# Rotating q and k in place in the attention loop of a decoder block, and moving one ScalarE copy

## The reference

```
x1 = layernorm(x  + mamba(x))                     # projection, causal conv, selective scan, gate, projection
x2 = layernorm(x1 + retention(x1, ctx))           # cross attention, no softmax
x3 = layernorm(x2 + experts(x2))                  # shared expert + top 2 of 8 routed experts
```

```
q = xpos(x1  @ Wq)                      # 256 features
k = xpos(ctx @ Wk, inverse_scale=True)
v = ctx @ Wv
scores = (q @ k.T) * decay_mask         # 128 x 128 in each sequence
out    = scores @ v

xpos(x) = x * cos_table + rotate_half(x) * sin_table
```

## Time and profile before

| | |
|---|---|
| time, median of 3 runs | 1811.83 us |
| profiled execution, its own time | 1807.94 us |
| its span in the profile | 1805.9 us |
| mean granted TensorE clock (share of 2.4 GHz) | 0.978 |
| PE busy | 1685.7 us (93%) |
| DVE busy | 1208.9 us (67%) |
| ACT busy | 805.4 us (45%) |
| POOL busy | 730.1 us (40%) |
| front stage | about 0 to 553 us |
| attention loop | about 553 to 1123 us |
| routed experts | about 1123 us to the end |

### The profile page before, as it was taken

One profiled execution on the slowest core, in us unless ns is written; L12 is line 12 of the kernel. 1 busy time (PEld: TensorE's weight loads), 2 busy tenths in 40 slices (PEclk: granted clock), 3 DMA queues, 4 the chain that ended last, 5 costly groups with the idle time before them and its releaser, 6 DMA issues.

```text
span 1805.9 us, 36443 instructions
## 1 busy us (share of the span) xinstructions
PE 1685.7 (93%) x9652; PEld 1434.9 (79%) x9653; DVE 1208.9 (67%) x2735; ACT 805.4 (45%) x1507; POOL 730.1 (40%) x673
## 2 busy tenths in 40 slices
PE   6999977999986999999999996999999999999995
PEld 4777746888875888888888874888888888888884
DVE  6888866788874676676677667555555555556554
ACT  5788856777732323323323324333333333333332
POOL 1111105888852345434435435233333333333333
PEclk9999988999998999999999998999999999999998
DMA  4555574778853232232233226334544444444444
GB/s 143 182 181 192 193 256 131 231 240 248 269 189 121 84 117 97 92 115 101 84 111 113 83 86 242 55 55 84 107 93 90 103 92 92 97 100 89 93 108 103
DMA packets 155373, 237.54 MB, mean 132 GB/s; under 512 B 41824, under 2 KB 119840, under 8 KB 146992
## 3 DMA queue, kind: packets, MB, share of 16 engines
q1 hardware_dynamic: 129728, 201.29, 34.4%
q0 software_dynamic: 25584, 35.54, 11.2%
HBM read 131.11 MB, written 105.64 MB: 131 GB/s over the span
## 4 chain that ended last, share of the span: by engine, by line
PE 56%; POOL 4%; issue 3%; DVE 3%; DMA 1%; ACT 1%; SPq 0%; POOLq 0%; ACTq 0%; DVEq 0%
PE block_banks L2873 21%; PE block_banks L2893 11%; PE block_banks L2772 5%; PE block_banks L2758 4%; PE block_banks L2882 3%; PE block_banks L2749 3%; POOL attention_turned_qk L2055 2%; PE block_banks L2675 2%; PE block_banks L2704 2%; PE block_banks L2861 2%; PE block_banks L2712 2%; POOL sorted L2044 1%; PE block_banks L2663 1%; PE block_banks L2693 1%; DVE back_w_down L2264 1%
## 5 line engine op out<-in xcount | busy, mean ns | idle before, releaser
L2873 PE MATMUL block_banks<-back_w_gu,back_xe_T 128*128 x1620 | 412.6, 403 | 4.8 <-DVE back_xe_T L2572 4.7
L2873 PEld LDWEIGHTS block_banks<-back_w_gu,back_xe_T 128*128 128x128 f32 x1620 | 297.4, 189 | 64.9 <-issue 5.6
L2893 PE MATMUL block_banks<-back_w_down,back_he_T 128*128 x1620 | 225.4, 288 | 1.5 <-DVE back_he_T L2584 1.5
L2893 PEld LDWEIGHTS block_banks<-back_w_down,back_he_T 128*128 128x128 f32 x1620 | 200.8, 188 | 1.8 <-issue 1.7
L1445 PE MATMUL block_banks<-front_xn_T,front_w_in_parts 128*128 128x512 f32 x768 | 187.9, 401 | 5.2 <-issue 3.3
L2087 POOL DMA_INDIRECT more<-back_y,back_token x67 | 103.9, 1551 | 216.5 <-DVE back_y L2591 198.6
L2044 POOL DMA_INDIRECT sorted<-back_x,back_slot x128 | 128.6, 1005 | 139.3 <-DVE back_slot L2389 91.2
L2087 POOL DMA_INDIRECT acc<-back_y,back_token x68 | 107.6, 1583 | 179.2 <-DVE back_y L2591 162.4
L1445 PEld LDWEIGHTS block_banks<-front_xn_T,front_w_in_parts 128*128 128x128 f32 x768 | 144.2, 191 | 42.5 <-issue 6.3
L1262 DVE SCALAR_TENSOR_TENSOR front_conv<-block_banks,front_conv_wb,front_conv 128x508 f32<-128x508 f32 (+2 forms) x192 | 140.8, 740 | 44.5 <-ACT front_conv L1075 38.6
L2223 ACT ACTIVATE back_he_T<-block_banks 128x512 fp32r<-128x512 f32 x135 | 80.8, 599 | 199.7 <-PE block_banks L2882 199.7
(11 more groups left out here) (267 smaller groups left out, 3113.3 us busy)
## 6 DMA issues: line engine op xcount, KB each, us to landing
back_xe<-sorted SPq DMA_DIRECT2D x135, 136.0 KB
gate_T<-front_gate_T SPq DMA_DIRECT2D x16, 1024.0 KB, 4.8
xc_T<-front_xc_T SPq DMA_DIRECT2D x16, 1024.0 KB, 5.8
front_xc_in<-xc_T SPq DMA_DIRECT2D x16, 1024.0 KB, 5.3
front_gate_in<-gate_T SPq DMA_DIRECT2D x16, 1024.0 KB, 6.6
front_x_rows<-in_x SPq DMA_DIRECT2D x16, 512.0 KB, 5.6
front_c_rep<-c_parts SPq DMA_DIRECT2D x128, 64.0 KB, 4.5
front_rows_in<-in_x SPq DMA_DIRECT2D x16, 512.0 KB, 7.7
```

What stands on the lines that cost most here:

```text
L2873: op = nc.tensor.matmul(dst[:, r % 2], xe_T[:, x_part, k], w_gu[:, bass.ds(e, 1), m, w_part, k], start=(n == 0), stop=(n == len(PASSES) - 1))
L2893: op = nc.tensor.matmul(ps_y[:, 0:D_MODEL], he_T[:, h_part, k], w_down[:, bass.ds(e, 1), w_part, k], start=(n == 0), stop=(n == len(DOWN_P ...
```

## The change

Two edits, both in the attention loop of `decoder_back`.

1. q and k each get two `parts` buffers of their own. DVE writes the two cosine products straight into `turned_qk`, where the sums are to stand, and the two sine products into `parts[2*which]` and `parts[2*which+1]`. POOL then adds or subtracts in place: `turned_qk` is an input and the output. DVE's wait for POOL's sums is now the same for q and k: those of the group before (`4 * a`). The wait for `scores_done` moves from POOL to DVE, which is now the first to write `turned_qk`.
2. On ACT, `chunk_high` moves from before the logits' copy to behind it.

```
@@ GpSimd, step @@
                     for which in range(0 if is_at(a, 0) else 2):
                         pool.wait_ge(parts_ready, 8 * a + 4 * which + 4)
-                        pool.wait_ge(scores_done, a)
                         for half, op in enumerate((ALU.subtract, ALU.add)):
-                            nc.gpsimd.tensor_tensor(turned_qk[:, which, half], parts[:, 2 * half], parts[:, 2 * half + 1],
-                                                    op).then_inc(xpos_ready, 1)
+                            nc.gpsimd.tensor_tensor(turned_qk[:, which, half], turned_qk[:, which, half],
+                                                    parts[:, 2 * which + half], op).then_inc(xpos_ready, 1)
@@ ScalarE, step @@
-                if expert and attention and u:
-                    chunk_high((g - 1) // 2)
-                if is_at(expert and g, GROUPS - 2):
-                    chunk_high(EARLY)
                 if is_at(expert and g, GROUPS - 1):
                     act.wait_ge(scores_done, GROUPS)
                     for c in range(8, 11):
...
                     nc.scalar.activation(logits_T, ps_small[0:2 * EXPERTS], ACT.Copy).then_inc(logits_T_ready, 1)
+                if expert and attention and u:
+                    chunk_high((g - 1) // 2)
+                if is_at(expert and g, GROUPS - 2):
+                    chunk_high(EARLY)
@@ VectorE @@
             def xpos_parts(a, which):
                 done, cos, sin = ((q_done, "q_cos", "q_sin"), (k_done, "k_cos", "k_sin"))[which]
-                dve.wait_ge(xpos_ready, 4 * a + 2 * which)
-                for i, half, table in ((0, 0, cos), (3, 0, sin), (1, 1, sin), (2, 1, cos)):
+                dve.wait_ge(xpos_ready, 4 * a)
+                dve.wait_ge(scores_done, a)
+                for dst, half, table in ((turned_qk[:, which, 0], 0, cos), (parts[:, 2 * which + 1], 0, sin),
+                                         (parts[:, 2 * which], 1, sin), (turned_qk[:, which, 1], 1, cos)):
                     dve.wait_ge(done, 2 * a + half + 1)
-                    nc.vector.tensor_tensor(by_seq(parts[:, i]), by_seq(ps_wide[:, half]), per_seq(tables[table]),
+                    nc.vector.tensor_tensor(by_seq(dst), by_seq(ps_wide[:, half]), per_seq(tables[table]),
                                             ALU.mult).then_inc(parts_ready, 1)
```

## The result

The changed kernel takes 1800.61 us (median of 7 runs, 1798.62 to 1806.36) against 1811.38 us for the kernel before in the same comparison (7 runs, 1809.32 to 1814.26). The ratio is 0.995, with a 95% interval from 0.9936 to 0.9963: 9.1 us less (6.7 to 11.6). On the 1811.83 us that the forecast started from, this is 1802.8 us. The forecast was 1804.0 us. The direction and the mechanism held; the size was too small, and what sits behind that size is the interesting part.

The account below looks back on a forecast made before the run. PE, busy 436.27 of 443 us in the attention loop, was taken to set the pace. Its waits, 3.1 + 2.6 + 2.1 = 7.8 us, off the median 1811.83 us gave 1804.0 us; range 1801 to 1809 us.

Parts of the forecast that it names:

- The waits at the logits, the score and the up projection: PE's only idle places in the attention loop from 604 to 1080 us: 3.1, 2.6 and 2.1 us, all to go.
- DVE's new wait for the scores: Before DVE writes the products, twice a step: claimed always met, since that score product starts over 20 us earlier.
- x1's low part: DVE's input to q's projection, ending 0.36 us before it: closest on PE, claimed to move forward with the removed waits.
- The slowed products of k: DVE's k products beside POOL's sums: at most 1.1 us each instead of 0.62, then ending at 787.33, as late as now.
- The term of the rotation: k's products no longer wait for POOL's sums of q; PE's score and up projection waits go: 2.6 + 2.1 = 4.7 us.
- The two starts agree with the idle time in brackets: Up projection to score: 1.90 us in an even step, 1.51 in an odd one, taken as without a wait; difference 0.39.
- Together 7.8 us. That is what there is to win: Sum of PE's listed idle time at three places in the attention loop, taken as all that could be won.
- the copy: ACT's logits' copy exchanged with a chunk's rounding in odd steps: PE's wait before the logits' transposes goes, 3.1 us.
- rival 1: One edit doesn't pay: k products slowed beside POOL, 1808.7 us; or the copy still waits, 1807.1 us. Chance 0.07 together.
- The second rival: Another PE wait in the loop takes their place, first x1's low part; if all is lost again, 1811.8 us. Chance 0.07.
- wrong on the sum if a new waiter stands in PE's list: The prediction's own sign against its 7.8 us: a new entry among PE's waits in the loop.
- What was to show it: Signs in the new profile: PE's three waits gone or each under 0.5 us, a middle step about 0.4 us less.

Follow-up runs that it names:

- the rotation alone: Edit to q/k buffers, in-place sums and DVE's waits, without moving ACT's chunk behind the logits' copy, against the kernel before: 1806.34 us, ratio 0.9968.
- the second profiles of the two kernels: Both kernels run again unchanged: the changed one 1803.05 us, ratio 0.9947 to the kernel before; a single run of the one before 1808.59 us.

## Why the prediction was right, and where its size was off

- **The places and the mechanism: right.** The waits at the logits, the score and the up projection went. The price in place is nil (1302 against 1304 ns), DVE's products and POOL's sums don't slow each other, DVE's new wait for the scores holds nothing, and x1's low part, the closest input by 0.36 us, never became a wait of PE. (The slowed products of k, which the paragraph on prices calls the second rival, are the first in the prediction's list.)
- **The term of the rotation: too small.** The step that failed is "The two starts agree with the idle time in brackets (1.90 - 1.51 = 0.39), so these are real gaps". They are real, but 1.51 us was taken as the distance without a wait, and that is 1.36: both steps waited. The score cost 0.26 us in an odd step and 0.64 in an even one, not 0 and 0.38 (by the lengths of the steps in the rotation alone, 0.2 and 0.7). The logits cost 0.52 us by the starts, for 0.45 in the bracket. A middle step without waits is 33.23 us, so the 13 steps had 442.94 - 13 x 33.23 = 10.9 us to win, and g = 14 another 1.1. "Together 7.8 us. That is what there is to win" was the lower bound.
- **The terms don't add as I added them.** Alone, the copy is worth nothing (0.9997) and the rotation 0.9968, which is 5.8 us; together 9.1. About 3 us belong to the copy only once the score no longer waits. So rival 1 had its prices wrong: with a rotation that doesn't pay, the copy would have given about nothing, not 1808.7 us.
- **The second rival came true in part, elsewhere.** A wait did take their place, at the router and not at x1; by the prediction's own sign ("wrong on the sum if a new waiter stands in PE's list") the sum was wrong. The router's input, x2's low part, had hardly more room than x1's: in step g = 6 before it ends at 782.93, and the router's product starts at 783.38. Of the 10.9 us, 3.7 were not won: three late steps at 1.0 to 1.1 us and one at 0.31 us at the router, and 0.19 us at the logits in g = 8. The router's wait was there before, where a late step cost 0.3 us; one profile without it made the loop look steadier than it is.
- **What was to show it.** A middle step was to lose about 0.4 us; it lost 0.72. The sums of k were to end over 1 us before the score; it is 1.2. The products of k were to start right behind x2's low part; PE's projection of k holds them for 0.33 us. "Behind the loop nothing should change": the last step grew by 1.71 us, at a DMA (0.89 us in the second profiles of the two kernels, 8.23 to 9.12).
- **The sum.** 10.9 + 1.1 - 3.7 us in the loop and 1.7 us given back behind it make 6.6; the profiled spans differ by 7.3, with 1.0 us by which the first middle step starts earlier (602.90 instead of 603.94; in the second profile of the changed kernel it is 604.74, so this is not the change's doing) and 0.4 us lost among the routed experts. That the forecast of 7.8 us came near the measured 9.1 is in part luck: two omissions of opposite sign, the score's and the logits' waits taken too small and the wait at the router and the longer last step left out.

## What to carry to other kernels

Take what a wait costs from the distance between two starts in a step that doesn't wait, not from the idle time in the list; where the awaited data are loaded as weights, look at the weight loads' waits too. Two waits in one step that hang on different engines are not to be priced apart: take the one away, and look at whether the other absorbs it. A second profile of the same kernel shows which waits come and go; slack that was covered by a removed wait is paid for in full from then on.

## What the runs showed of the hardware

- Behind the jump back of a loop whose body is two pairs of steps, DVE stood still for 4.00 and 4.38 us, each time beside transfers of instructions. With a body of one pair no instructions are transferred from 704 to 1048 us. Written out, the kernel fetches steadily (24 transfers of instructions in that stretch) and PE waits for none of it.
- In the one-pair loop PE's second count on `x2_turned` came up to 2.3 us behind the modelled end of its transposes, in the first step of some turns, and up to 0.8 us in odd steps; in the written-out kernels it was never more than 0.7 us behind.
- DVE with one input in PSUM and one in SBUF runs beside POOL's sums at no cost for either (0.68 us, 2.57 us).
